# A fused cross-attention and feed-forward kernel: values product moved behind two projection products, VectorE and ScalarE steps reordered

## The reference

```python
h = layernorm(x)                                   # 8 batches, 128 tokens, 512
h_q = (rmsnorm(h, ln_weight) @ w_q.T)              # 512 -> 32 heads x 128
h_k = (ctx @ w_k.T)
h_v = (ctx @ w_v.T)
score = softmax(where(mask, h_q h_k^T + position_bias, -inf))
score = where(mask, score, 0)
x = x + h + (score h_v) @ w_out.T                  # 32 heads x 128 -> 512
```

## Time and profile before

| | us |
|---|---|
| median of 3 runs | 1052.1 |
| lowest, highest | 1050.58, 1052.56 |
| the profiled execution | 1051.31 |
| its span in the profile | 1049.5 |
| PE busy in it | 945.6 |
| DVE, ACT, POOL busy | 693.6, 681.1, 520.7 |
| mean granted PE clock | 0.982 of full |

### The profile page before, as it was taken

How to read it: one execution, slowest core, us unless ns; L and a number is a source line. 1 busy time by engine, 2 the same in 40 slices (tenths; PEclk the granted TensorE clock), 3 DMA queues, 4 the chain that set the end, 5 groups by cost and what they waited for, 6 DMA issues and landing times.

```text
span 1049.5 us, 17500 instructions
## 1 busy us (share of the span) xinstructions
PE 945.6 (90%) x5261; PEld 800.1 (76%) x5261; DVE 693.6 (66%) x1225; ACT 681.1 (65%) x2103; POOL 520.7 (50%) x582
## 2 busy tenths in 40 slices
PE   9989999898889889988999799988998888889998
PEld 8778888787778777877788687777786776668885
DVE  5565864666766475766675776657665767748787
ACT  5777766675767666755776666756666666734565
POOL 2440635464547445564457345755466452204477
PEclk9989999999999999999999999999999999989999
DMA  9123437644656265745563556526563554320001
GB/s 329 67 86 121 149 149 275 216 146 141 246 205 217 86 227 188 254 140 195 200 218 117 196 189 236 189 91 238 196 226 138 200 186 156 108 110 1 32 21 61
DMA packets 61292, 171.71 MB, mean 164 GB/s; under 512 B 6055, under 2 KB 8491, under 8 KB 60988
## 3 DMA queue, kind: packets, MB, share of 16 engines
q1 hardware_dynamic: 61244, 171.11, 46.8%
HBM read 159.56 MB, written 11.53 MB: 163 GB/s over the span
## 4 chain that ended last, share of the span: by engine, by line
PE 47%; ACT 16%; DVE 16%; issue 12%; POOL 7%; DMA 0%; DVEq 0%; SPq 0%; ACTq 0%; POOLq 0%
ACT probs_t L798 10%; PE ps_t L2194 4%; PE ps_q L363 4%; PE ps_k L363 3%; PE ps_k L364 3%; PE ps_k L365 3%; PE ps_q L364 3%; PE ps_q L365 3%; PE ps_v L363 3%; PE ps_s L2173 2%; PE ps_o L363 2%; PE ps_v L365 2%; PE ps_v L364 2%; ACT scores L787 2%; DVE scores L1607 2%
## 5 line engine op out<-in xcount | busy, mean ns | idle before, releaser
L798 ACT COPY probs_t<-scores 32x128 f32<-32x128 f32 x1024 | 303.1, 296 | 111.5 <-DVE scores L1610 99.7
L363 PE MATMUL ps_o<-wo_hi,att_hi 128*128 128x512 f32 x256 | 106.8, 417 | 43.2 <-DVE att_lo L1472 22.1
L787 ACT ACTIVATE scores<-scores,neg_max 128x128 f32<-128x128 f32 x256 | 99.8, 391 | 52.1 <-DVE neg_max L1598 51.7
L1484 DVE TENSOR_TENSOR acc<-ps_o,acc 128x512 f32<-128x512 f32 x128 | 86.0, 672 | 57.5 <-PE ps_o L365 57.3
L781 ACT CAST att_hi<-ps_t 128x512 fp32r<-128x512 f32 x64 | 37.5, 586 | 109.1 <-PE ps_t L2194 109.0
L1159 POOL TENSOR_TENSOR wq_lo<-raw_q,wq_hi 128x256 fp32r<-128x256 f32 x65 | 47.8, 736 | 111.7 <-ACT wq_hi L620 111.6
L365 PE MATMUL ps_o<-wo_hi,att_lo 128*128 128x512 f32 x256 | 101.1, 395 | 0.0
L364 PE MATMUL ps_o<-wo_lo,att_hi 128*128 128x512 f32 x256 | 101.0, 395 | 0.0
L363 PEld LDWEIGHTS ps_o<-wo_hi,att_hi 128*128 128x128 f32 x256 | 48.4, 189 | 67.9 <-issue 30.0
L1118 POOL TENSOR_TENSOR shift<-bias_sb,mask_sb 128x512 f32<-128x512 f32 x64 | 84.0, 1315 | 2.7 <-DVE scores L1594 2.7
L363 PE MATMUL ps_v<-wv_hi,ct_hi 128*128 128x256 f32 x264 | 77.3, 293 | 1.2 <-DVE vv L1438 0.9
(11 more groups left out here) (393 smaller groups left out, 2835.4 us busy)
## 6 DMA issues: line engine op xcount, KB each, us to landing
ring_hi<-scratch_x_t SPq DMA_DIRECT2D x39, 512.0 KB, 3.9
ring_lo<-scratch_x_t SPq DMA_DIRECT2D x39, 512.0 KB, 4.9
ring_hi<-scratch_c_t SPq DMA_DIRECT2D x39, 512.0 KB, 4.1
ring_lo<-scratch_c_t SPq DMA_DIRECT2D x39, 512.0 KB, 5.2
raw_o<-in_w_o SPq DMA_DIRECT2D x16, 512.0 KB, 3.3
raw_q<-in_w_q SPq DMA_DIRECT2D x15, 512.0 KB, 6.1
raw_k<-in_w_k SPq DMA_DIRECT2D x15, 512.0 KB, 7.0
xt_hi<-scratch_x_t SPq DMA_DIRECT2D x13, 512.0 KB, 8.2
```

The source lines that it names most:

```text
L363: pe.matmul(dst, hi_l, hi_r, start=first, stop=False)
L787: e = act.activation(probs[n][:, m, :], scores[n][:, m, :], ACT.Exp, bias=neg_max[:, n, m:m + 1], accum_out=row_sum[:, n, m:m + 1])
L798: last = act.copy(block_of(probs_t, j, i), block_of(scores[n], i, j))
L1484: dve.tensor_tensor(acc[:, b, :], ps_o[:], acc[:, b, :], ALU.add).then_inc(o_added, 1)
```

## The change

The same instructions are run, in another order on PE, DVE and ACT; POOL's and SP's order stay. On PE each step is now: scores, two units (in some steps a unit and a v half), PV, then the rest. The v halves that stood behind an output half move forward: v_p3 and v_p4 right behind PV, v_p6 and v_p7 (first halves) ahead of O1, their second halves ahead of the next PV. On ACT the exponentials stand ahead of `att_hi` of the step before; the copies q_first, k_first, v_first are set around them. On DVE the addition of O1 and the sums of projections move behind the maximum of the next step, `attention_rest` behind those, and the transposition is taken out of `softmax_back` (`turn_blocks`), so that in steps 3 and 7 an addition and sums stand between the multiply and the transposition. `v_p4` gets one more wait for its input block. The core of the diff, ACT:

```diff
+                exponentials(s, s % 2)
                 if s > 0:
                     attention_high(s - 1)
-                exponentials(s, s % 2)
...
-                attention_high(s - 1)
                 if c % 4 == 2 and more:
                     k_first(G)
+                exponentials(s, n)
+                if c == 4 and coming:
+                    v_first(i + 1, 0)
+                if c % 4 == 1 and more:
+                    q_first(G)
+                attention_high(s - 1)
                 if c % 4 == 3 and more:
                     high_fourth(G)
-                exponentials(s, n)
...
                 if c == 4 and coming:
-                    v_first(i + 1, 0)
                     high_v2(i + 1)
+                    v_first(i + 1, 1)
...
                 pt_blocks(s, n, (0, 1))
-                if c == 4 and coming:
-                    v_first(i + 1, 1)
```

DVE, the part of a step from the maximum to the transposition in the new order (all lines moved, none new but `turn_blocks`):

```diff
+                softmax_front(s, n)
...
+                add_output(s - 2, (c - 2) % LOOP_STEPS, (1,))
...
                 if c % 4 == 3:
                     q_u3(G)
+                if c == 3:
                     k_u3(G)
-                    q_c21(G)
...
+                if c == 3 and own:
+                    v_c21(i, 0)
...
+                attention_rest(s - 1)
+
+                if c == 7:
+                    k_c11(G)
+                if c == 3:
+                    q_c21(G)
                 softmax_back(s, n)
-                add_output(s - 1, (c - 1) % LOOP_STEPS, (0,))
+                if c % 4 == 3:
+                    add_output(s - 1, (c - 1) % LOOP_STEPS, (0,))
+                    if c == 7:
+                        k_u3(G)
+                        q_c21(G)
+                    k_c21(G)
+                turn_blocks(s, n)
...
+                if c % 4 != 3:
+                    add_output(s - 1, (c - 1) % LOOP_STEPS, (0,))
```

PE:

```diff
             def v_p4(p, h):
+                if h == 0:
+                    pe.wait_ge(ring_in[2], 128 * p - 48)
...
                 step_scores(s, c)
+
+                if c % 4 == 0:
+                    q_p5(g)
+                    k_p5(g)
+                if c == 0:
+                    q_p3(g)
+                if c == 4 and coming:
+                    v_p1(i + 1, 0)
+                if c % 4 == 1 and more:
+                    q_p1(G)
+                    q_p6(G)
+                if last and c == 5:
+                    q_p3(g)
+                if c == 6:
+                    v_p6(i + 1, 1)
+                if c % 4 == 2:
+                    q_p7(G)
+                if c == 2:
+                    q_p2(G)
+                if c == 7:
+                    v_p7(i + 1, 1)
+                if c % 4 == 3:
+                    q_p4(G)
+
                 if c == 0:
                     step_values(s - 1, 7, v_count(i - 1, 14))
...
                         v_p4(i, 0)
...
+                    k_p4(G)
...
+                if c == 7:
+                    k_p2(G)
+                output(s - 1, (c - 1) % LOOP_STEPS, g if c % 4 == 1 else None, (0,))
+
+                if c == 0:
+                    v_p5(i, 1)
...
+                if c == 5 and coming:
+                    v_p6(i + 1, 0)
+                if c == 6:
+                    v_p7(i + 1, 0)
+                if c == 7:
+                    k_p4(G)
...
                 output(s - 1, (c - 1) % LOOP_STEPS, None, (1,))
```

More of the change, by code:

```diff
@@ L929, in _ @@
             wq1_high_part(3)
-            attention_high(STEPS - 3)
             def mm_high(m):
@@ L1614, in step_first @@
                 softmax_front(s, n)
-                if s > 0:
-                    attention_rest(s - 1)
+                if s > 1:
+                    add_output(s - 2, (s - 2) % LOOP_STEPS, (1,))
                 if s == 0:
@@ L1678, in step @@
                 coming = not last
[L1679 to L1686, removed]
+                if c % 4 == 1 and summed and not (last and c == 5):
+                    q_c12(g)
+                if c == 3:
+                    k_c11(G)
+                if c == 6 and coming:
+                    v_u2(i + 1, 0)
+                if c == 7 and coming:
+                    v_u3(i + 1, 0)
+                softmax_front(s, n)
+                if c == 0 and own:
+                    v_u3(i, 1)
+                if c == 1 and own:
+                    v_c22(i, 1)
+                    v_u4(i, 1)
                 if c == 4 and not last:
@@ L1691, in step @@
                         v_evac(13, 2, 1, done=16)
[L1692 to L1701, removed]
+                if c == 5 and coming:
+                    v_c11(i + 1, 0)
+                add_output(s - 2, (c - 2) % LOOP_STEPS, (1,))
                 if c % 4 == 0 and summed:
@@ L1733, in step @@
                         v_evac(14, 3, 0, done=13)
+                if c % 4 == 2:
+                    q_c11(G)
                 if c == 2 and own:
                     v_c12(i, 1)
-                if c == 3 and own:
-                    v_c21(i, 0)
                 if last and c == 4:
                     v_c21(i, 1)
[L1740 to L1745, removed]
                 if c % 4 == 0 and summed:
@@ L1748, in step @@
                     k_u4(g)
+                if c % 4 == 1 and more:
+                    q_u2(G)
                 if isinstance(i, int) and s == FIRST:
                     block_low(1, wide[0], 7)
[L1751 to L1759, removed]
                 if last and c == 5:
-                    wq1_rest(2)
+                    k_c12(g)
+                    for m in range(3):
+                        wq1_rest(m)
             def target_experts():
@@ L1852, in _ @@
             softmax_front(STEPS - 2, 0)
+            add_output(STEPS - 4, 4, (1,))
             attention_rest(STEPS - 3)
+            softmax_back(STEPS - 2, 0)
+            turn_blocks(STEPS - 2, 0)
             add_output(STEPS - 3, 5, (0,))
-            softmax_back(STEPS - 2, 0)
             weighted_rows(1, [wk1_raw[:, c, :] for c in range(NC)], 0)
@@ L2411, in step @@
                     step_values(s - 1, c - 1, v_count(i, (1, 2, 11, 12, 13, 14, 14)[c - 1]))
[L2412 to L2451 removed]
+                if c == 0:
+                    v_p5(i, 0)
+                    k_p3(g)
                 if c == 1:
@@ L2496, in step @@
                     v_p4(i, 1)
+                if c == 4 and coming:
+                    v_p2(i + 1, 0)
+                    k_p3(g)
+                if c == 5 and coming:
+                    v_p6(i + 1, 0)
+                if c == 6:
+                    v_p7(i + 1, 0)
+                if c == 7:
+                    k_p4(G)
+                if last and c == 5:
+                    pe.wait_ge(v_out, v_count(i, 14))
+                    for _ in range(4):
+                        pe.matmul(ps_v[:, 0:P], ones[:], ones[:], start=True, stop=True)
+                output(s - 1, (c - 1) % LOOP_STEPS, None, (1,))
+                if c == 1 and not own:
+                    step_v(15, 13, PLAIN)
             for c in range(1, LOOP_STEPS):
```

116 lines of the change are left out of this document (39 added, 77 removed).

## The result

The changed kernel takes 1125.9 us (median of 4 runs, 1123.4 to 1127.0) against 1052.3 for the kernel before, measured beside it: a ratio of 1.070, 95% interval 1.067 to 1.072. The forecast was 1081 with a range from 1060 to 1102: the direction was right, the size was not.

What follows compares the result with a forecast made beforehand. No one engine was taken to bound the turn. Legs 116.1 plus clock 2.2 gave 118.3 us, 5.8 over the mean; five turns 29, outside 0: 1051.3 + 29 = 1080, against the median 1081, range 1060 to 1102.

Steps and rivals of the forecast that it cites:

- The four waits for wv_lo: PE waiting for late values weights in each turn: about 3.5 us in step 1, 5 in step 3, 3 in step 5, 4 in step 6.
- step 3: Chain from the values product of step 3 to that of step 4: 18.5 us, where the same leg took 12.0.
- the last sign: Sign in the new profile that the forecast is right: looping turns of 116 to 120 us.
- The legs: One chain through a looping turn, from values product to values product, summed over eight steps: 116.1 us against 113.1.
- step 5: Chain from the values product of step 5 to the next: 15.8 us, with 4.78 to the first copy.
- steps 0 and 1 together: Chain through steps 0 and 1, over the end of v_p3's weight and the products behind it: 27.6 us.
- steps 4 and 7: Chains from the values products of steps 4 and 7 to the next: 14.2 and 13.8 us.
- The clock: Lost PE clock behind waits in looping turns: 2.2 us a turn, with ends at 0 and 6.8.
- rival 1: PE's clock falls at every one of the four waits: 122.9 us a turn, 1104 us for the run; chance 0.10.
- Outside the loop: First eight steps gain 0 to 5 us, turn before the loop and last turn lose 0 to 8: set at 0.
- rival 2: Faster, as DVE's softmax passes are no longer stretched: 1015 to 1049 us, likeliest 1043; chance 0.21.
- rival 3: Nothing changes, every chain arrives as before and waits only change names: 1050 to 1054 us; chance 0.06.

Runs made afterwards that it cites:

- two casts earlier: The changed kernel with all four values weights earlier, plus the weight casts of q_p7 and k_p7 set between the two halves of the copies: 1001.3 us, ratio 0.951.

## Why the prediction was too low

**The mechanism was right.** The four waits for wv_lo were put at 3.5, 5, 3 and 4 us and came at 3.49, 3.99, 3.43 and 4.23; together 15.5 forecast, 15.1 measured. v_p4 was to start about 5 us behind PV of step 3, it does at 5.15. The first copy was to come over 4.5 us behind PV in steps 5 and 6: it comes 6.2 and 4.8 behind. Turns of 116 to 120 us, the last sign, did not come: they take 123.9.

**The legs** were summed to 116.1 us at full clock; with the clock held up by spare matmuls a turn takes 116.96. That this is so near is in part luck, since errors cancel: in that run, from PV to PV, step 5 is 1.5 us over its 15.8, steps 0 and 1 together and step 3 are 0.4 over, and steps 4 and 7 are 1.0 and 0.6 under. The leg that was short is that of step 5: in the changed kernel the first copy comes 475.06 - 468.87 = 6.19 us behind PV, not 4.78. ACT, and then DVE, in that step:

```profile
469.73 0.40 ACT L787 ACTIVATE scores<-scores,neg_max 128x128 f32<-128x128 f32 x1 [2.52 <-DVE neg_max L1598]
...
471.76 0.58 ACT L781 CAST att_hi<-ps_t 128x512 fp32r<-128x512 f32 x1
...
475.06 2.45 ACT L798 COPY probs_t<-scores 32x128 f32<-32x128 f32 x8 [2.73 <-DVE scores L1612]
```

```profile
467.88 1.82 DVE L1598 TENSOR_SCALAR neg_max<-row_max 128x4 f32<-128x4 f32 x1
```

The exponentials stand ahead of att_hi and begin at 469.73, behind the start of PV, as the maximum's negative took 1.82 us; q_first follows them, and att_hi starts 2.89 us behind PV instead of 1.10. I had charged the exponentials in step 3 alone, with 0.5. Why the negative took so long there no run told apart.

**The clock is the term that failed.** I took 2.2 us a turn, what the kernel before loses, "as the nearest row"; it is 6.9, the upper end that I had set for rival 1 (6.8) and given a chance of 0.10. The mistake was to carry a price per turn to a turn with other waits, where the windows behind 490.48 gave a price per wait. Four waits longer than the one that had already lost the clock were forecast, and each should have been charged 1.7. That four times 1.7 then meets 6.9 so closely is in part luck too: in the second looping turn the clock stays at 1.00 behind step 5's wait, and behind step 6's it is 0.50 through the whole window. The Trainium skill ("TensorE: Matmul & The Clock Gate", HAM oscillation — how this bites in real kernels) says that a loop whose waits are long enough loses the clock in every pass. The trace agrees for three of the four waits of that turn and not for the one of step 5. In the forecast I set the rule aside on the strength of one turn at clock 1.00. In the loop the clock makes (6.9 - 2.2) x 5 = 23.5 us, the legs 0.86 x 5 = 4.3. With 6.9 for the clock the forecast would have been 1104.5, rival 1's number, and still 21 us short.

**Outside the loop** I set gains and losses against each other at 0; it is 15.6 more. The first eight steps do gain (2.6 us), but the turn ahead of the loop loses 6.4, and from the last turn on 11.8 are lost. Most of it is late weights and clock: with the weights in time the same stretches take 17.5 us less, some 2 less than before. Of the 11.8, though, 4.5 stay, and no run told what they are.

These are all but 1.5 us of the miss: 1081 + 23.5 + 4.3 + 15.6 = 1124.4, against 1125.9.

**The rivals.** DVE's passes did not shorten (rival 2): from reciprocal to first copy the changed kernel takes 2.1 to 3.1 us in the steps where no sums stand between, against the 1.87 to 2.41 read before. Nothing changed (rival 3) was out of the question. What no rival held is that the order is good and only the supply late: 36 us faster with six calls, for four weights, in other places.

## What to carry to other kernels

When work is moved forward on the engine that bounds the kernel, move what feeds it too, and look for the engine's idle time right ahead of the place where the feed now stands: here POOL and ACT had it, and moving a few calls there turned 7% slower into 5% faster. A wait of several microseconds on PE has two prices, the wait and the half clock behind it; charge the second per wait. Here it was 1.7 us for each of the four on average, and nothing for some. Spare matmuls in a wait measure that second price while nothing is made earlier.

## What was not expected of the hardware

The length of a wait alone did not tell whether the clock falls. A wait of 3.43 us in step 5 was followed by clock 1.00 in the second looping turn, while in the fourth the wait of the same step, 3.42 us, was followed by 0.63:

```profile
726.00:730.00 4.00, 2.35 (x11) 2.36 (x12) 0.00 (x0) 3.87 (x14) 2.11 (x3) 0.63 0.00 0
```

One of 2.3 us in the kernel with four early weights was followed by 0.50 (its window from 394.00). With no wait over 1.1 us left in the turn, the clock was 1.00 in all five turns of the run with spare matmuls, and so it was with waits of 1.5 us left (two casts earlier).
